# Last batch of a fused LoRA and stream-mixing kernel: mixing by block products instead of per-stream terms

## What is computed

```python
cond = einsum('bsi,boi->bso', x, weight[ids])          # 512 x 2048 by 2048 x 2048
norm = cond * rsqrt(mean(cond * cond) + eps)
H_res = sinkhorn(norm @ W_res.T + base, 50 rounds)     # 4 x 4 matrix of each token
H_res = (1 - g) * I + g * H_res                        # g = sigmoid(gate)
H_pre, H_post = softmax(norm @ W_pre.T + ..), softmax(norm @ W_post.T + ..)
y = einsum('btnc,btn->btc', cond, H_pre) @ W_branch
out = x + einsum('btij,btjc->btic', H_res, cond) + einsum('btc,btn->btnc', y, H_post)
```

## Time and profile before

| | |
|---|---|
| median of 3 runs | 1774.47 us (1774.23 to 1777.13) |
| profiled execution | 1779.6 us, span 1777.8 us |
| busy share of the span | PE 95%, DVE 84%, ACT 40%, POOL 5% |
| last product of batch 8 ends | about 1636.8 us |
| scaling on DVE | 1650.4 to 1701.0 and 1705.7 to 1739.1 us |
| matrix ready | 1739.9 us |
| last DVE term ends, last store issued | 1774.6, 1774.7 us |

### The profile page before, as it was taken

The page is one execution under the profiler, slowest core; times in us unless marked ns, Lnnn a source line. Parts: engine busy times, 40 slices in busy tenths (PEclk is TensorE's granted clock), DMA queues, the critical chain, the costliest instruction groups (busy, mean ns, idle before and its releaser), DMA issues.

```text
span 1777.8 us, 24362 instructions
## 1 busy us (share of the span) xinstructions
PE 1682.2 (95%) x7690; PEld 1358.4 (76%) x7690; DVE 1488.3 (84%) x6016; ACT 709.5 (40%) x1143; POOL 95.8 (5%) x96
## 2 busy tenths in 40 slices
PE   9999999999999999999999999999999999999704
PEld 8888888877888788887888878887888878887601
DVE  4323599888999799987999889996999879997999
ACT  4334433343344534253343533344342543433503
POOL 0000000000000000000000000000000000000504
PEclk9999999999999999999999999999999999999857
DMA  6223323383244733475234832556234753347002
GB/s 231 93 93 132 131 95 107 107 256 135 95 120 149 233 104 107 107 209 176 90 106 120 261 129 84 128 167 213 97 107 112 212 174 95 107 135 233 1 1 94
DMA packets 65073, 237.72 MB, mean 134 GB/s; under 512 B 7344, under 2 KB 7472, under 8 KB 64816
## 3 DMA queue, kind: packets, MB, share of 16 engines
q1 hardware_dynamic: 56880, 206.80, 34.1%
q0 software_dynamic: 8064, 29.36, 9.2%
HBM read 202.58 MB, written 33.55 MB: 133 GB/s over the span
## 4 chain that ended last, share of the span: by engine, by line
PE 82%; DVE 13%; DMA 4%; ACT 1%; issue 0%; SPq 0%; ACTq 0%; DVEq 0%
PE acc L1016 71%; PE y_ps L1073 4%; DMA x_raw<-xt 3%; DVE piece L886 3%; PE turn_ps L1031 3%; DVE work L829 2%; DVE x_raw L912 2%; PE logit_ps L1039 2%; PE logit_ps L1042 2%; DVE vec L827 1%; DVE vec L825 1%; DVE x_lo L658 1%; DVE w_lo L650 1%; ACT x_hi L412 1%; PE y_ps L1063 1%; PE turn_ps L1051 0%
## 5 line engine op out<-in xcount | busy, mean ns | idle before, releaser
L1016 PE MATMUL acc<-w_hi,x_hi 128*128 128x512 f32 x2048 | 812.6, 397 | 3.7 <-ACT acc L428 2.7
L1016 PE MATMUL acc<-w_hi,x_lo 128*128 128x512 f32 x2048 | 799.5, 390 | 0.0
L1016 PE MATMUL acc<-w_lo,x_hi 128*128 128x512 f32 x2048 | 798.2, 390 | 0.0
L1016 PEld LDWEIGHTS acc<-w_hi,x_hi 128*128 128x128 f32 x2048 | 385.3, 188 | 85.5 <-issue 5.4
L1016 PEld LDWEIGHTS acc<-w_hi,x_lo 128*128 128x128 f32 x2048 | 384.9, 188 | 82.9
L1016 PEld LDWEIGHTS acc<-w_lo,x_hi 128*128 128x128 f32 x2048 | 385.6, 188 | 76.7
L405 ACT ACTIVATE w_hi<-w_raw 128x1024 fp32r<-128x1024 f32 x256 | 270.4, 1058 | 382.9 <-DMA w_raw<-wt 382.6
L650 DVE TENSOR_TENSOR w_lo<-w_raw,w_hi 128x1024 fp32r<-128x1024 f32 x256 | 311.7, 1218 | 108.9 <-ACT w_hi L405 108.2
L886 DVE SCALAR_TENSOR_TENSOR piece<-cond,kern,piece 128x512 f32<-128x512 f32 x448 | 304.1, 746 | 0.0
L829 DVE TENSOR_TENSOR work<-kern,vec 128x32 f32<-128x32 f32 x1536 | 250.5, 202 | 0.0
L827 DVE RECIPROCAL vec<-vec 128x8 f32<-128x8 f32 x1536 | 239.8, 198 | 0.0
(11 more groups left out here) (110 smaller groups left out, 799.0 us busy)
## 6 DMA issues: line engine op xcount, KB each, us to landing
w_raw<-wt SPq DMA_DIRECT2D x256, 512.0 KB, 3.5
x_raw<-xt SPq DMA_DIRECT2D x64, 512.0 KB, 6.1
piece<-xn POOLq DMA_DIRECT2D x56, 512.0 KB, 7.0
out<-piece SPq DMA_DIRECT2D x56, 512.0 KB, 4.7
x_raw<-xn SPq DMA_DIRECT2D x8, 512.0 KB, 6.3
out<-x_raw SPq DMA_DIRECT2D x8, 512.0 KB, 2.6
cond<-wb SPq DMA_DIRECT2D x1, 1024.0 KB, 15.4
cond<-wall SPq DMA_DIRECT2D x1, 192.0 KB, 13.4
```

The source lines that it names most:

```text
L1016: mm = nc.tensor.matmul(acc[t][:], stationary, moving, start=(chunk == 0 and m == 0), stop=(chunk == CHUNKS - 1 and m == 2))
```

## The change

The residual x of the last batch is loaded, and the result stored, in another layout: partition 32 i + k holds stream i of token k of a group of 32 tokens. A tile has four such groups, so there are again 16 planes of 128 x 512, but a plane now is (tile, token group). `group_cond` on SP copies `cond` into this layout (`grouped`, in the place of `x_hi`) with 16 DMAs of 32 partitions. With this layout the four terms of all four streams of 32 tokens are one product with a 128 x 128 block matrix (`mix_group`). Its entries come from `kern`: PE spreads them over the partitions (`spread_matrix`), DVE selects and places them (`block_of`). The base of each plane is made in PSUM during the scaling: `ident` times x plus a block of H_post times y (`sum_base`), copied back to `end_out` by ACT (`copy_base`). DVE adds the product to it (`add_base`). POOL does no arithmetic any more: the low part of the branch input is made by PE, which subtracts the high part in PSUM (`take_pre`), and a second ACT copy. Loads and stores of the last batch are four DMAs of 32 partitions where one of 128 partitions was, with rows of 2 KB for 4 KB. Constants (`select`, `same_token`, `same_stream`, `minus_ident`) are made in batch 0, and the scratch of the software DMA is halved to make room.

```diff
...
+        grouped = nc.alloc_sbuf_tensor_at("grouped", [P, GROUPS, TILES, C], F32,
+                                          offset=nc.sbuf_base - CHUNKS * TOKENS * 4)
...
+        select = sb("select", [P, GROUPS, STREAMS, GROUP])
+        same_token = sb("same_token", [P, GROUP])
+        same_stream = sb("same_stream", [P, STREAMS])
+        spread_kern = sb("spread_kern", [P, GROUPS, TILES * STREAMS, STREAMS])
+        own_kern = sb("own_kern", [P, GROUPS, TILES * STREAMS])
+        minus_ident = sb("minus_ident", [P, P], F32R)
         end_out = x_raw
         end_c, end_term = cond[:, 1, :, :, :], cond[:, 0, :, :, :]
...
+        mix_block = w_raw[:, 0:2, :, :].rearrange("p s k c -> p (s k c)").rearrange(
+            "p (t g m) -> p t g m", g=GROUPS, m=P)
+        y_block = w_raw[:, 2:4, :, :].rearrange("p s k c -> p (s k c)").rearrange(
+            "p (t g m) -> p t g m", g=GROUPS, m=P)
+        y_sb = piece[:].rearrange("p s e c -> p (s e) c")
...
-        end_bank = acc + [y_ps[0]]
+        end_bank = acc + y_ps
...
             def load_last_residual(q):
                 wait_unit(sp, BATCHES - 1, 3 * PASS_UNITS + q)
-                sp.dma_start(end_out[:, 2 * q:2 * q + 2, :], rows(xn, (BATCHES - 1) * MIX_PAIRS + q)
-                             ).then_inc(x_in[q], 16)
+                (t, h), half = divmod(q, 2), 2 * GROUP
+                for i in range(STREAMS):
+                    p, s = divmod(i, 2)
+                    sp.dma_start(end_out[i * GROUP:(i + 1) * GROUP, 2 * q:2 * q + 2, :],
+                                 xn[(BATCHES - 1) * MIX_PAIRS + 2 * t + p,
+                                    h * half:(h + 1) * half, s * C:(s + 1) * C]
+                                 .rearrange("(e k) c -> k e c", e=2)).then_inc(x_in[q], 16)
+            def group_cond(j):
+                if j == STREAMS - 1:
+                    sp.wait_ge(cond_ready, BATCHES * STREAMS * TILES)
+                for g in range(GROUPS):
+                    sp.dma_start(grouped[j * GROUP:(j + 1) * GROUP, g, :, :],
+                                 cond[g * GROUP:(g + 1) * GROUP, 1, j, :, :]
+                                 ).then_inc(cond_grouped, 16)
+            def store_planes(t, first, number):
+                rows_of = slice(first * GROUP, (first + number) * GROUP)
+                planes = slice(t * GROUPS + first, t * GROUPS + first + number)
+                sp.wait_ge(out_ready, t * GROUPS + first + number)
+                for i in range(STREAMS):
+                    p, s = divmod(i, 2)
+                    sp.dma_start(out[(BATCHES - 1) * MIX_PAIRS + 2 * t + p, rows_of,
+                                     s * C:(s + 1) * C].rearrange("(g k) c -> k g c", g=number),
+                                 end_out[i * GROUP:(i + 1) * GROUP, planes, :]
+                                 ).then_inc(stored_last, 16)
             def ending():
                 store(BATCHES - 2, MIX_PAIRS - 1)
                 load_last_residual(MIX_PAIRS - 1)
...
+                sp.wait_ge(acc_done, BATCHES * STREAMS * TILES)
+                for j in range(STREAMS):
+                    group_cond(j)
+                for t in range(TILES - 1):
+                    store_planes(t, 0, GROUPS)
+                store_planes(TILES - 1, 0, GROUPS // 2)
+                store_planes(TILES - 1, GROUPS // 2, GROUPS // 2)
...
-            def ending():
-                first_tile = (BATCHES - 1) * TILES
...
-            ending()
...
                     nc.scalar.activation(xpre_t[:, 0, :], y_ps[t % 2][:], ACT.Copy
                                          ).then_inc(pre_hi_ready, 1)
-                    if t > 0:
-                        act.wait_ge(pre_lo_ready, first_tile + t)
-                    nc.scalar.activation(xpre[:], y_ps[t % 2][:], ACT.Copy
-                                         ).then_inc(pre_copied, 1)
+                    act.wait_ge(pre_taken, t + 1)
+                    nc.scalar.activation(xpre_t[:, 1, :], y_ps[t % 2][:], ACT.Copy
+                                         ).then_inc(pre_lo_ready, 1)
...
-                def weigh_y(t):
+                def spread_post(t):
+                    for i in range(STREAMS):
+                        weigh(y_block[:, t, :, i * GROUP:(i + 1) * GROUP], select[:, :, i, :],
+                              logit[:, t, NRES + STREAMS + i:NRES + STREAMS + i + 1],
+                              y_block_ready)
+                def copy_y(t):
                     act.wait_ge(y_ready, first_tile + t + 1)
...
+                    nc.scalar.activation(y_sb[:, t, :], acc[t][:], ACT.Copy
+                                         ).then_inc(y_copied, 1)
+                def copy_base(n):
+                    act.wait_ge(base_summed, n + 1)
+                    nc.scalar.activation(end_out[:, n, :], end_bank[n % len(end_bank)][:],
+                                         ACT.Copy).then_inc(base_ready, 1)
...
+                    if t == 0:
+                        for slot in range(OUT_SLOTS):
+                            act.wait_ge(stored[slot], (BATCHES - 1) * 2 * 16)
                     if t > 0:
-                        weigh_y(t - 1)
-                weigh_y(TILES - 1)
+                        copy_y(t - 1)
+                copy_y(TILES - 1)
                 answer_log_step(asks, 1)
-                act.wait_ge(matrix_ready, 1)
-                for n in range(len(END_TENSOR)):
-                    for j in range(STREAMS):
-                        diagonal(n, j)
-                        if n * STREAMS + j < END_GPSIMD_TERMS:
-                            term(n, j)
-                    if n > 0:
-                        copy_sum(n - 1)
-                copy_sum(len(END_TENSOR) - 1)
+                for t in range(TILES):
+                    spread_post(t)
+                for n in range(END_PLANES):
+                    copy_base(n)
...
+                        act.wait_ge(ident_ready, 1)
+                        nc.scalar.activation(minus_ident[:], ident[:], ACT.Copy, scale=-1.0
+                                             ).then_inc(minus_ready, 1)
...
+                by_stream = ident[:].rearrange("p (j k) -> p j k", j=STREAMS)
+                nc.vector.tensor_reduce(same_stream[:], by_stream, AX, ALU.add
+                                        ).then_inc(masks_ready, 1)
+                nc.vector.tensor_reduce(same_token[:], ident[:].rearrange(
+                    "p (j k) -> p k j", j=STREAMS), AX, ALU.add).then_inc(masks_ready, 1)
+                nc.vector.tensor_copy(select[:], by_stream.unsqueeze(2).to_broadcast(
+                    [P, GROUPS, STREAMS, GROUP])).then_inc(masks_ready, 1)
...
-                    for group in END_VECTOR:
-                        dve.wait_ge(base_added, max(t * STREAMS + i for t, i in group) + 1)
...
+                    dve.wait_ge(kern_spread, 1)
+                    dve.wait_ge(masks_ready, 3)
+                    link(tt(spread_kern[:], logit_ps[:, 0:GROUPS * TILES * NRES].rearrange(
+                        "p (g f j) -> p g f j", g=GROUPS, j=STREAMS),
+                            same_stream[:].unsqueeze(1).unsqueeze(1).to_broadcast(
+                                [P, GROUPS, TILES * STREAMS, STREAMS]), ALU.mult))
+                    link(reduce(own_kern[:], spread_kern[:], AX, ALU.add))
+                    def block_of(t):
+                        weights = own_kern[:, :, t * STREAMS:(t + 1) * STREAMS]
+                        tt(mix_block[:, t, :, :].rearrange("p g (i k) -> p g i k", i=STREAMS),
+                           weights.unsqueeze(3).to_broadcast([P, GROUPS, STREAMS, GROUP]),
+                           same_token[:].unsqueeze(1).unsqueeze(1).to_broadcast(
+                               [P, GROUPS, STREAMS, GROUP]), ALU.mult
+                           ).then_inc(mix_block_ready, 1)
+                    def add_base(n):
+                        dve.wait_ge(base_ready, n + 1)
+                        dve.wait_ge(block_mixed, n + 1)
+                        tt(end_out[:, n, :], end_bank[n % len(end_bank)][:], end_out[:, n, :],
+                           ALU.add).then_inc(out_ready, 1)
+                    block_of(0)
+                    for t in range(TILES):
+                        if t + 1 < TILES:
+                            block_of(t + 1)
+                        for g in range(GROUPS):
+                            add_base(t * GROUPS + g)
...
+                def take_pre(t):
+                    pe.wait_ge(minus_ready, 1)
+                    pe.wait_ge(pre_hi_ready, first_tile + t + 1)
+                    nc.tensor.matmul(y_ps[t % 2][:], minus_ident[:], xpre_t[:, 0, :],
+                                     start=False, stop=True, skip_group_check=True
+                                     ).then_inc(pre_taken, 1)
+                def sum_base(n):
+                    t, bank = n // GROUPS, n % len(end_bank)
+                    pe.wait_ge(x_in[n // 2], (BATCHES + STREAMS) * 16)
```

(83 more changed lines are left out.)

91 lines of the change are left out of this document (13 added, 78 removed).

## The result

| | before | after |
|---|---|---|
| median | 1775.8 us (4 runs, 1774.2 to 1779.3) | 1754.2 us (4 runs, 1752.7 to 1755.9) |
| span of the profiled execution | 1777.8 us | 1750.6 us |
| start of the ending (first weighing on ACT) to matrix ready | 90.9 us | 76.1 us |
| matrix ready to the last term or add on DVE | 34.7 us | 20.1 us |
| from there to the end | 3.2 us | 8.0 us |

The account below looks back on a forecast made before the run. DVE's chain, then one store, was taken to bound the ending. Span 1777.8 - 14.8 (scaling) - 37.9 + 31.1 (matrix to end) = 1756.2; less 3.3 from span to median, forecast 1752.9 us, range 1742 to 1760.

Parts of the forecast that it names:

- POOL held DVE's multiplies: First scaling: without POOL, its 96 multiplies fall from 31.7 to 14.6 us, 17.1 us less.
- ACT is late next: Second logarithmic step: DVE waits for ACT, 2.5 of the 17.1 us not got; matrix 14.8 us earlier.
- The base is hidden: Second scaling: PE's base products take 29.6 us, end 4.3 us ahead of the matrix, cost zero.
- Rival (b): Second scaling: PE stays at half clock, base ends at 1746, time 1769 to 1774 us; chance 0.06.
- From the matrix to the first product: After the matrix: `spread_matrix`, DVE's selection, reduce and first block put 3.2 us on the path.
- The slow records of the products: Mixing: five of 32 PE records at half clock, 4.3 us, in 15.9 us of products.
- The stores set the end: Kernel's end: 2 KB packets cost as much as 4 KB, so 207 GB/s, 20.3 us for 4.19 MB.
- rival (a): Kernel's end: stores run at full rate, 414 GB/s; span 1748.1, time 1744.8 us; chance 0.29.
- Nothing for the scratch: Accumulating loads of POOL in all batches: halving the software DMA's scratch costs zero.
- The constants: Batch 0: three DVE operations and one ACT copy cost zero, at most 2 us.
- Small DMAs do overlap: Final stores: more than one DMA's latency can be under way, against 2.6 us for each of 20 stores.
- Rival (d): Final stores: small DMAs do not overlap, 52 us for 20 stores, time 1783.3 us; chance 0.04.

Follow-up runs that it names:

- pool_adds: Changed kernel with 20 POOL additions of 128x512, on a buffer nobody reads, during the first scaling; 1767.6 us.
- early_take: Changed kernel with two buffers for the high part and `take_pre` of a tile ahead of the turn of tile t+2 on PE; ratio to before 0.9853.
- again: The changed kernel once more, unaltered, beside the store variants on the same chip; ratio to before 0.9886.
- keep_warm: Changed kernel with five more matmuls, result unread, on PE between the base and the matrix; ratio to before 0.9860.
- full_2k: Changed kernel with last-batch stores as one DMA of 128 partitions, rows of 2 KB, other output order in DRAM; ratio to before 0.9854.
- quarter_8k: Changed kernel with four store DMAs of 32 partitions kept, but rows of 8 KB (4 KB in the last tile); ratio to before 0.9883.
- half_stores: Changed kernel with stores as two DMAs of 64 partitions, rows of 2 KB; 269 GB/s in the mean, end 7.3 us after the last add.
- full_8k: Changed kernel with stores of 128 partitions and rows of 8 KB (4 KB in the last tile); ratio to before 0.9847.
- scratch_only: Kernel before with only the software DMA's scratch halved; ratio to before 0.9991.
- alternating: Changed kernel with a tile's four stores in stream order 0, 2, 1, 3; 280 GB/s, end 6.6 us after the last add.

## Why the prediction was right, and where it was not

From the start of the ending, the forecast was 107.1 us (1756.2 less 1649.06) and 104.2 were measured.

1. **POOL held DVE's multiplies.** Right, in cause and size: 31.7 to 14.8 us, and pool_adds brings 13.2 of these 16.9 us back.
2. **ACT is late next.** Right: an idle time of 2.33 us where 2.5 was worked out, and the matrix at 76.1 us where 76.0 was. (My gain of 14.8 us is not 17.1 less 2.5, which is 14.6: it counts from 1701.17, when ACT began, and 2.5 from 1700.96.) In other traces of the same code the wait was up to 3.4 us and the matrix came at up to 77.2. early_take shows that the order was the reason, `take_pre` behind `turn_terms` together with ACT's copies.
3. **The base is hidden.** Right: PE was done 4.7 us ahead of the matrix (forecast 4.3). Rival (b) did not come: the clock rose 3.6 us after the first record, and the 64 records took 29.5 us (forecast 29.6).
4. **From the matrix to the first product** 3.8 us, forecast 3.2. The term that was too small is `spread_matrix`: 1.87 us, nearly all at the half clock, where I had taken 1.1 to 1.5, although my own price (3.73 us for 32, twice that at the half clock) gives 1.87 for 8. The slow records of the products cost less than forecast, 1.6 us (5.28 less 3.67) for 2.1. So the last add at 20.1 us, for 19.9, is met in part because two errors cancel. Both terms hang on when the clock falls and rises: in again `spread_matrix` took 1.10 us and the slow records cost 2.5, with the last add at 20.3. keep_warm prices both together at 2.4 us.
5. **The stores set the end.** Right that they do, wrong in the reason. I chose the lower rate because I held the number of packets to be what counts. full_2k refutes it, quarter_8k shows the other side, and half_stores points to the ports of SBUF. The size was off as well: from the first store to the end 18.3 us (1732.3 to 1750.6) and not 21.6, for the rate is 255 GB/s, not 207. The rows of before had no DMA of fewer than 128 partitions, so they could not tell the two apart. The rule of the Trainium skill, page SBUF — State Buffer, section "Door 1: The DMA port swizzle", which I had put in a sentence of its own, was the better reason, but not the better number: at its 196 GB/s for one DMA the stores would take 21.4 us, and the 20 stores here took 18.3 us. On full rate, rival (a), the end comes 1751.8 - 1652.3 = 99.5 us after the start of the ending, as full_8k shows; my working had 99.0.
6. **Nothing for the scratch.** Right, by scratch_only. The constants were not tried alone.
7. **Small DMAs do overlap.** Rival (d) is refuted: 20 stores within 18.3 us, with landings of 2.2 to 4.6 us.

That the median was met within 1.3 us is luck. The forecast span, 1756.2 us, is 5.6 us longer than the 1750.6 of the trace: 2.9 us within the ending, where the stores were priced 3.3 us too high, and 2.7 us because this trace began its ending earlier than that of before. The step from span to median went the other way by more. I subtracted 3.3 us, as the profiled execution of before was slower than its median, while the median of after lies 3.6 us above its profiled span. That the reduction was met to 0.1 us is luck too: the traces show 24.5 us in the ending, for 21.6 forecast, and the interval of the ratio reaches from 18.6 to 25.4 us.

## What to carry to other kernels

A second engine that reads SBUF beside a chain of short two-input VectorE instructions can cost more than it computes: look for one line whose mean differs between two stretches, and at who else is busy there. When work is moved to block products, price the relayout of loads and stores too: a DMA that touches only partitions below 64 or only those above lost about a third of the rate here (250 to 280 GB/s against 371 and more), and if it is the last thing in the kernel, that shows in the time. Before a burst on TensorE that ends the kernel, a few matmuls in its idle time kept the clock up here and saved 2.4 us.

## What the runs showed of the hardware

- Stores of 32 or 64 partitions ran at 250 to 280 GB/s in the mean of their store time (quarter_8k, alternating), with 211 and 344 in single microseconds of half_stores. Those of 128 ran at 371 to 387 with rows of 2 KB and at 393 to 426 with rows of 8 KB (4 KB in the last tile). Copies from 32 to 32 partitions within SBUF ran at 212 GB/s.
- SP itself is held when such DMAs queue: an issue in `group_cond` took 1.04 us in the median, against 0.33 to 0.38 for the stores of the earlier trace rows. The last stores of 32 partitions were issued at 1747.8, 5.2 us after the last add.
- POOL additions (in the kernel before also subtractions) of 128x512 that read SBUF cost DVE's 128x32 multiplies 0.66 to 0.85 us each, while memsets of the same size cost nothing.
- PE's clock stayed up through a pause of 1.84 us behind a busy stretch (keep_warm). It fell at 1722.6 in the changed kernel, 4.8 us after the last record of the base, at 1720.9 in early_take, only 2.4 us after it, and at 1725.4 in again, 5.3 us after it.
